# Second modulation, spectrum sums, last residual and shared product of the last batch on VectorE, with a new slot order

## The reference

```python
scores = jnp.einsum('bthd,bghd->bhtg', Q, K) / np.sqrt(DH)
topv, topi = jax.lax.top_k(scores, K_TOP)          # 32 of 1024, 4 heads
attn_mean = attn.mean(axis=1);  c_t = attn_mean @ V
x = layernorm(x_text, g_norm_in, b_norm_in)
x = x * (1.0 + mod_gate * scale_in) + mod_gate * shift_in      # "film in", from c_t
y = s4d(x, ...)                                                # long convolution by FFT
y = y * (1.0 + mod_gate * scale_out) + mod_gate * shift_out    # "film out"
xt = x_text + y
xt = xt + gelu(layernorm(xt, g_ffn, b_ffn) @ W1 + b1) @ W2 + b2
...                                                            # layernorm, then x + tanh(g) * (that)
top_id = jnp.argmax(x @ gate_w); score = sigmoid(max)          # 8 experts, one for each row
y = (silu(xs @ rt_gate[e]) * (xs @ rt_up[e])) @ rt_down[e]     # xs = x * score
shared = (silu(x @ sh_gate) * (x @ sh_up)) @ sh_down
x = x + tanh(g_ffn) * (shared + routed)
```

## Time and profile before

| | us |
|---|---|
| median of 3 runs | 1805.63 |
| lowest, highest | 1803.59, 1806.4 |
| the profiled execution | 1804.41 |
| its span (first to last instruction) | 1802.6 |

### The profile page before, as it was taken

The page is one execution under the profiler, slowest core; times in us unless marked ns, Lnnn a source line. Parts: engine busy times, 40 slices in busy tenths (PEclk is TensorE's granted clock), DMA queues, the critical chain, the costliest instruction groups (busy, mean ns, idle before and its releaser), DMA issues.

```text
span 1802.6 us, 20762 instructions
## 1 busy us (share of the span) xinstructions
PE 1409.9 (78%) x6269; PEld 987.7 (55%) x6269; DVE 1479.2 (82%) x2091; ACT 1111.9 (62%) x2366; POOL 1204.7 (67%) x1349
## 2 busy tenths in 40 slices
PE   6566658778876878679878878897788778878796
PEld 3233445455544555547565646564656465655796
DVE  7999999999999999889998999899989993103121
ACT  3689844856485648555976587658864775233442
POOL 1499838577856885697678958895789568515232
PEclk8666778879887988799999999898989989988898
DMA  7200120012102200122232222232223210843232
GB/s 214 59 5 2 39 68 31 24 45 56 25 12 49 50 24 7 47 83 76 76 83 65 73 72 71 62 88 74 59 65 87 55 53 22 266 121 105 62 51 27
DMA packets 96451, 115.16 MB, mean 64 GB/s; under 512 B 17840, under 2 KB 73144, under 8 KB 96196
## 3 DMA queue, kind: packets, MB, share of 16 engines
q1 hardware_dynamic: 84196, 99.26, 19.0%
q0 software_dynamic: 12144, 14.58, 5.1%
HBM read 75.48 MB, written 19.58 MB: 53 GB/s over the span
## 4 chain that ended last, share of the span: by engine, by line
DVE 52%; PE 15%; POOL 12%; issue 11%; ACT 7%; DMA 3%; SPq 1%; POOLq 0%; DVEq 0%
DVE R L1419 18%; DVE ZB L1422 15%; DVE ZB L1415 6%; DVE R L1411 6%; PE PS L1952 3%; DVE R L1376 2%; DMA out<-R 2%; ACT ZB L1009 2%; POOL ZB L725 2%; POOL R L904 2%; ACT R L1015 2%; PE PS L2063 2%; POOL R L898 1%; POOL xs_d L882 1%; PE PS L1971 1%
## 5 line engine op out<-in xcount | busy, mean ns | idle before, releaser
L1419 DVE MAX8 R<-ZB 128x8 f32<-128x1024 f32 x384 | 471.3, 1227 | 12.2
L1422 DVE MATCH_REPLACE8 ZB<-R,ZB 128x1024 f32<-128x1024 f32 x384 | 464.1, 1209 | 0.0
L1012 ACT ACTIVATE R<-PS 128x512 f32<-128x512 f32 (+6 forms) x412 | 181.8, 470 | 193.6 <-PE PS L2017 32.2
L725 POOL TENSOR_TENSOR ZB<-ZB 128x1024 f32<-128x1024 f32 x96 | 231.6, 2413 | 94.6 <-ACT ZB L1009 90.8
L727 POOL TENSOR_TENSOR ZB<-ZB 128x1024 f32<-128x1024 f32 x96 | 226.5, 2359 | 7.5
L1009 ACT ACTIVATE R<-R 128x32 f32<-128x32 f32 (+4 forms) x356 | 96.4, 275 | 196.9 <-DVE R L1419 172.1
L1411 DVE MAX8 R<-PS 128x8 f32<-128x1024 f32 x128 | 156.2, 1220 | 1.2 <-PE PS L1705 1.2
L1415 DVE MATCH_REPLACE8 ZB<-R,PS 128x1024 f32<-128x1024 f32 x128 | 155.4, 1214 | 0.0
L1015 ACT ACTIVATE R<-R 128x1 f32<-128x1 f32 (+1 forms) x384 | 140.7, 391 | 20.2 <-POOL R L712 15.2
L1009 ACT ACTIVATE ZB<-ZB,R 128x1024 f32<-128x1024 f32 x128 | 146.2, 1143 | 0.3 <-DVE ZB L1422 0.2
L1009 ACT ACTIVATE ZB<-PS,R 128x1024 f32<-128x1024 f32 x128 | 142.6, 1114 | 4.2
(11 more groups left out here) (247 smaller groups left out, 3048.1 us busy)
## 6 DMA issues: line engine op xcount, KB each, us to landing
ZR<-ZR SPq DMA_DIRECT2D x96, 128.0 KB
ZB<-in_L_ffn_rt_gate SPq DMA_DIRECT2D x21, 512.0 KB, 4.1
ZB<-in_L_ffn_rt_up SPq DMA_DIRECT2D x21, 512.0 KB, 5.0
ZB<-in_L_ffn_rt_down SPq DMA_DIRECT2D x21, 512.0 KB, 6.3
R<-in_x SPq DMA_DIRECT2D x16, 512.0 KB, 4.9
ZB<-in_ctx SPq DMA_DIRECT2D x8, 768.0 KB, 5.4
R<-xs_d SPq DMA_DIRECT2D x39, 128.5 KB, 2.2
out<-R SPq DMA_DIRECT2D x32, 128.0 KB, 1.7
```

The lines of the kernel that those rows point to most:

```text
L725: pool.tensor_tensor(e, e, w, ALU.subtract).then_inc(s.g_att, 1)
L1012: return act.activation(o, i, ACT.Copy, **k)
L1419: vec.max(ml[:, 8 * r:8 * r + 8], w).then_inc(s.v_tk, 1)
L1422: vec.match_replace(w, ml[:, 8 * r:8 * r + 8], w, NEG).then_inc(s.v_tk, 1)
```

## The change

For the last batch alone, POOL's film in, fold, spectrum sums, inverse sums, film out, residual and shared product are written into VectorE's program instead. They stand at the slots `DVE_LAST`. The shared product then reads its second factor out of PSUM, so ACT's four copies of it go; PE's SH_DOWN waits for these products by the banks that they free. The other batches keep the work on POOL. Besides, every slot table of every engine has new numbers; of these the diff shows five. Lines of the changed kernel are 1 to 3 higher up to 1544 and up to 69 higher behind.

```diff
-POOL_OUT = ((101, 101, 101.9, 102.8), (88.7, 88.8, 89.1, 89.3))
...
+POOL_OUT = (92.2, 92.2, 92.4, 95.2)
...
-ACT_SH = ((134.2, 135, 145.6, 145.6), (134, 134, 138.1, 161.5))
...
+ACT_SH = ((146.9, 147.4, 147.4, 147.7), (143, 161.7, 161.7, 161.7))
...
-DVE_ROUTE = ((118.3, 119.4), (123.3, 123.3))
...
+DVE_ROUTE = ((121.2, 123.6), (109.4, 112.3))
...
+DVE_LAST = (4, 8.5, 13.1, 28.9, 28.9, 45.2, 45.2, 45.2, 46, 46, 46, 47.2, 47.2, 50.2, 50.2, 82.4, 88.7, 88.7, 89.4, 132.3,
+            133.9, 133.9, 141)
...
+                    if b < B - 1:
+                        for i in range(4):
+                            yield at + POOL_FILM_IN[i]
...
+                    if b < B - 1:
+                        for i in range(4):
+                            yield at + POOL_OUT[i]
...
             def shared():
-                for b in range(B):
+                for b in range(B - 1):
                     for k in range(4):
-                        yield post_at(b) + POOL_SHUP[b == B - 1][k]
+                        yield post_at(b) + POOL_SHUP[k]
                         use = SHARED + 4 * (k // 2) + k % 2
...
+                    if b == B - 1:
+                        for i in range(4):
+                            yield at + DVE_LAST[i]
+                            fi = big[:, 4 + i, :]
+                            on.wait_ge(*q_done("post", b, FILM_IN + i))
+                            on.wait_ge(s.a_ln, 12 * b)
+                            for k in range(4):
+                                on.wait_ge(s_res[k], 16 * b)
+                            on.wait_ge(s.g_fi, n)
+                            t = own.then_inc(TT(u[:, i, :], xl[:, i, :], fi[:, 0:256], ALU.mult))
+                            on.wait_ge(own.sem, t)
+                            TT(u[:, i, :], u[:, i, :], fi[:, 256:512], ALU.add).then_inc(s.g_fi, 1)
+                        yield at + DVE_LAST[4]
+                        on.wait_ge(s.g_fi, n + 4)
+                        for i in range(4):
+                            on.wait_ge(s_acc[i], 16 * b)
+                        own.then_inc(TT(xt[:, 0:2, :], u[:, 0:2, :], u[:, 2:4, :], ALU.add))
+                        TT(xt[:, 2:4, :], u[:, 0:2, :], u[:, 2:4, :], ALU.subtract).then_inc(s.g_sd, 1)
                     for j in range(4):
                         yield at + DVE_SPECTRUM[b == B - 1][j]
...
+                        if b == B - 1:
+                            yield at + DVE_LAST[5 + j]
+                            on.wait_ge(*q_done("post", b, DFT + j))
+                            on.wait_ge(*q_run("post", b - 1, SH_DOWN + 3))
+                            on.wait_ge(s.g_y, n)
+                            own.then_inc(TT(yf[:, j, 0:256], q0[:, 0:256], q1[:, 256:512], ALU.subtract))
+                            TT(yf[:, j, 256:512], q0[:, 256:512], q1[:, 0:256], ALU.add).then_inc(s.g_y, 1)
...
+                    if b == B - 1:
+                        for i in range(2):
+                            yield at + DVE_LAST[9 + i]
+                            on.wait_ge(*q_done("post", b, INV + i))
+                            on.wait_ge(s.g_inv, n)
+                            TT(xt[:, i, :], qs[i][:, 0:256], qs[i][:, 256:512], ALU.add).then_inc(s.g_inv, 1)
+                            TT(xt[:, i + 2, :], qs[i][:, 0:256], qs[i][:, 256:512], ALU.subtract).then_inc(s.g_inv, 1)
+                        for i in range(4):
+                            yield at + DVE_LAST[11 + i]
+                            fo = big[:, i, :]
+                            on.wait_ge(*q_done("post", b, FILM_OUT + i))
+                            on.wait_ge(s.g_inv, n + 4)
+                            t = own.then_inc(TT(xt[:, i, :], xt[:, i, :], fo[:, 0:256], ALU.mult))
+                            on.wait_ge(own.sem, t)
+                            TT(xt[:, i, :], xt[:, i, :], fo[:, 256:512], ALU.add).then_inc(s.g_fo, 1)
                     yield at + DVE_MOMENTS[b == B - 1][0]
...
+                    if b == B - 1:
+                        for i in range(4):
+                            yield at + DVE_LAST[15 + i]
+                            z = tmp[i][:, 0:D]
+                            on.wait_ge(s.a_ln, 12 * b + 4 + i + 1)
+                            on.wait_ge(s.a_w, 4)
+                            on.wait_ge(s.g_z, n)
+                            t = own.then_inc(TT(z, z, gout, ALU.mult))
+                            on.wait_ge(own.sem, t)
+                            t = own.then_inc(TT(z, z, bout, ALU.add))
+                            on.wait_ge(own.sem, t)
+                            on.wait_ge(s.xr_in, 16 * b + 16)
+                            TT(x1[:, i, :], z, u[:, i, :], ALU.add).then_inc(s.g_z, 1)
...
+            def shared():
+                b = B - 1
+                for k in range(4):
+                    yield post_at(b) + DVE_LAST[19 + k]
+                    use = SHARED + 4 * (k // 2) + k % 2
+                    on.wait_ge(*q_done("post", b, use))
+                    on.wait_ge(*q_run("post", b, use + 2))
+                    TT(big[:, k, :], big[:, k, :], q_bank("post", b, use + 2), ALU.mult).then_inc(q_sem("post", b, use + 2), 1)
...
-            weave(setup(), attention(), prep(), weights(), kernel_rows(), post(), tiles(), routed())
+            weave(setup(), attention(), prep(), weights(), kernel_rows(), post(), shared(), tiles(), routed())
...
-                        on.wait_ge(s.g_sh, 4 * b + 4)
+                        if b < B - 1:
+                            on.wait_ge(s.g_sh, 4 * b + 4)
+                        else:
+                            for use in (2, 3, 6, 7):
+                                on.wait_ge(*q_done("post", b, SHARED + use))
```

More of the change, by code:

```diff
@@ L811, in post @@
-                    yield at + POOL_FOLD[b == B - 1][0]
-                    on.wait_ge(s.g_fi, 4 * b + 4)
-                    for i in range(4):
-                        on.wait_ge(s_acc[i], 16 * b)
-                    own.then_inc(pool.tensor_tensor(xt[:, 0:2, :], u[:, 0:2, :], u[:, 2:4, :], ALU.add))
-                    pool.tensor_tensor(xt[:, 2:4, :], u[:, 0:2, :], u[:, 2:4, :], ALU.subtract).then_inc(s.g_sd, 1)
-                    for j in range(4):
-                        yield at + POOL_SPECTRUM[b == B - 1][j]
-                        q0, q1 = qs[2 * (j % 2)], qs[2 * (j % 2) + 1]
-                        on.wait_ge(*q_done("post", b, DFT + j))
-                        if b:
-                            on.wait_ge(*q_run("post", b - 1, SH_DOWN + 3))
-                        own.then_inc(pool.tensor_tensor(yf[:, j, 0:256], q0[:, 0:256], q1[:, 256:512], ALU.subtract))
-                        pool.tensor_tensor(yf[:, j, 256:512], q0[:, 256:512], q1[:, 0:256], ALU.add).then_inc(s.g_y, 1)
@@ L1322, in shared @@
             def shared():
-                for b in range(B):
+                for b in range(B - 1):
                     for k in range(4):
-                        yield post_at(b) + ACT_SHUP[b == B - 1][k]
+                        yield post_at(b) + ACT_SHUP[k]
                         use = SHARED + 4 * (k // 2) + k % 2 + 2
```

222 lines of the change are left out of this document (112 added, 110 removed), and 8 rows, old and new, of the table POST_AT.

## The result

The changed kernel is slower: 1821.39 us median (1820.57 to 1823.29, four runs) against 1804.61 (1803.36 to 1806.4), a ratio of 1.0094 with a 95% interval of 1.0076 to 1.0111. I had forecast 1793, with 0.07 for slower. The profiled execution has a span of 1819.7 where it had 1802.6.

The account below looks back on a forecast made before the run. VectorE (82% busy) was taken to bound attention to 1507 us, then a chain through all engines. Main part -4.4 and tail -8.0 gave -12.4 from 1802.6, forecast 1793; own range 1788 to 1796, overall 1784 to 1801.

Parts of the forecast that it names:

- step 1: Route in batches 0 and 1: later gate and rank groups cover VectorE's waits of 2.15 and 1.24; -5.6 us.
- The rule that I set aside: GpSimd and VectorE share SBUF access, holding up two-SBUF-input instructions; would make the last residual 1.3 longer, left out.
- step 2: Batches 2 to 5, routing tables on POOL: sum 14 ahead of scaling starts 0.7 later per frame; net -0.3 us.
- Other slots: Main part, remaining slots moved by an instruction or two, first frame above all: +0.8 us, bounds -2 and +3.
- Rival C: Three POOL residual biases ahead of a sum wait for ACT's late tiles, stalling VectorE in seven frames: 1820, chance 0.08.
- The tail: Last batch after attention, work moved from POOL to VectorE: the end comes 8.0 us earlier.
- The fold: Tail, after the accumulate lands: on VectorE two adds take 1.4 to 1.5 with handoff instead of 2.64; -1.1 us.
- The residual: Tail, last residual: twelve adds take 5.5 on VectorE instead of 8.7 on POOL; -3.3 us at the second moments.
- Root and gate: Tail: ACT's last SiLU moves earlier, to just behind the moments, so root and gate come 7.0 us earlier.
- The shared part: Tail, shared product on VectorE: SH_DOWN waits less, though two matmul pairs need a freed bank; -3.5 us, bounds 0 and -5.5.
- rival D: Shared matmuls keep the higher clock throughout with fewer pauses ahead: 1788 us, chance 0.11.
- The late accumulates: Tail: three copies behind ACT's weight pick put three accumulates in a row before the first expert scatter: +2.5 us.

Follow-up runs that it names:

- run 5: Changed kernel with the route's gate group rewritten to read first operands from PSUM, intermediates in the gate's bank, no tensor_scalar: 1800.46 us, ratio 0.9967 to before.
- main_new: Kernel before with the changed kernel's slots for batches 0 to 6, old slots and old POOL work for the last batch: 1828.88 us, ratio 1.0121.
- route_late: Kernel before with only VectorE's route slots (DVE_ROUTE) of batches 0 to 6 set to the changed kernel's later ones: 1829.13 us, ratio 1.0125.
- gate_early: Changed kernel with the gate group of batches 0 to 6 back three attention instructions earlier, rank group left: 1819.73 us, ratio 1.0079.
- psum_route: Changed kernel, gate group computed from PSUM with fused compare-and-multiply operations, some tensor_scalars still reading SBUF: 1823.21 us, ratio 1.0089.
- probe_two: Kernel before plus one 128x8 VectorE add, both operands in SBUF, behind each attention tile's first MATCH_REPLACE8: 1866.83 us, one run.

## Why the prediction was wrong

1. **Route, step 1: the mechanism was half of it.** The waits went as forecast (3.4 a frame in batches 0 and 1, and their like later). The two groups of a route then took 5.6 in three frames and 6.8 in four, in place of 2.5 to 2.8. In batches 0 to 2 that leaves 0.3 to 0.6 of the 3.4 gained; in batches 3 to 5, which had 1.3 to 2.0 of wait to lose, the route costs 2.0 to 2.4 each. I had priced the moved instructions at their old durations. The step that failed is that one: "both should be covered by 1.2 us instructions". I asked what stood ahead of them on VectorE, not what POOL would run beside them at the new time. In its place the runs show two operations of each group held to the end of POOL's sum, 26.5 us in seven frames, and 21.0 us back once the gate group no longer had two operands in SBUF (run 5).
2. **The rule that I set aside.** The rule of the GPSIMD Engine Reference (section Specifications) in the Trainium skill, which names VectorE instructions with two SBUF inputs, or in a 2-port mode, stood in the prediction, weighed only for the tail's adds, where POOL has nothing to run and they did cost 0.42 to 0.43 (0.69 for the fold). The place where it decides was the main part, where POOL's order had just been moved as well. I priced it at 1.3 us, left that out of the sum, and it cost about 20. The row that I priced it by was misread too. The nine adds at 41.53 are not slowed to 0.56 each: the first lasts 1.36, since POOL's L795 runs to 42.61, and the eight behind it 0.43 each, with POOL idle. The merged row hid a hold behind a mean.

```profile
41.53 1.36 DVE L1376 TENSOR_TENSOR R<-R 128x256 f32<-128x256 f32 x1
```

```profile
41.29 1.32 POOL L795 TENSOR_TENSOR ZR<-R,ZR 128x512 fp32r<-128x512 f32 x1 [10.93 <-ACT R L1012]
```

3. **Tables, step 2.** The wait for POOL's last sum was forecast at about 17 and is 21.6. The new order of sum and scaling cost 1.4 to 1.8 in each of three frames where I had 0.7. Part is the hold again: in run 5 these intervals are 0.7 to 1.1 shorter.
4. **Other slots.** I took 0.8. In run 5, with most of the hold gone, attention ends 1.6 after that of before, where the forecast had it 4.4 ahead: 6.0 for everything else, of which the 4.7 of hold that is left there can be a part. That is also most of what run 5 lacks: it is 5.6 faster than before where I forecast 12.4. The intervals of the changed kernel show 3.8 in the first 16 tiles, 1.3 at the spectrum's products in two frames, 1.2 to 1.7 for PE's routed tile in three. How much of the first is the order and how much the start, which moved by 1 to 2 between executions, is open.
5. **Rival C, the L845 trio,** is real and small. The slack of 3.43 at that sum fell to 0.83, as the 2.7 that I charge say, and never below nothing. In one frame of seven a wait for a sum came one tile further on, L1418 for L726, 2.70.
6. **From the last route to the fold.** The landing of the last accumulate came 27.0 late (1567.05 after 1540.01) where attention was 19.6 late. The last route begins 26.9 late (1518.74 after 1491.87), since its gate group stands 1.1 behind the last tile's first MATCH_REPLACE8 where it stood 6.2 ahead. From there to the landing it is 48.3, before 48.1; without the hold at the gate group, in run 5, 44.6.
7. **The tail came as forecast or better.** Starts in the profiled executions, with `main_new` as the fair comparison (the same main part, the old tail):

| start of | before | changed | `main_new` | changed less `main_new` | forecast |
|---|---|---|---|---|---|
| DFT | 1542.7 | 1568.5 | 1568.3 | +0.2 | -1.1 |
| UP | 1582.6 | 1606.2 | 1608.3 | -2.1 | -1.6 |
| gate | 1644.4 | 1664.8 | 1669.9 | -5.0 | -7.0 |
| SH_DOWN | 1675.8 | 1688.8 | 1701.3 | -12.5 | -10.5 |
| first expert tile | 1686.8 | 1699.3 | 1712.2 | -12.9 | -10.5 |
| first scatter | 1712.7 | 1728.1 | 1739.7 | -11.5 | -8.0 |
| end | 1802.6 | 1819.7 | 1828.9 | -9.2 | -8.0 |

The accumulates landed 1.5 later in the changed kernel's execution than in that of `main_new` (1567.05, 1565.59). Counted from the landing each difference is 1.5 larger: 1.2 less at the DFT, 6.5 at the gate, 10.7 at the end.

The fold is 1.3 long and 1.5 with the handoff, as priced. The residual's twelve adds take 6.2 in place of 8.7; the last normalised tile comes 1.0 late behind a copy that waits for PE. The root begins right behind the SiLU, as forecast, and the SiLU came 0.9 after the moments' end where I had 0.3. (Root and gate are 6.6 by my own working, 1635.89 less 1629.3; I wrote 7.0.)

The shared part gained 7.5 between gate and SH_DOWN where I had 3.5, and the four more have a cause that I had not seen. VectorE must finish the route's tables before it takes the first product. It is free 18.7 after the gate matmul begins, in the kernel before 23.1. Of these 4.5, 2.9 are the held 128x1 add shown above: the seven adds take 1.32 where they took 4.19, since POOL has no shared products left to hold them. `main_new` has such a hold as well, 2.55 for an operation of 0.49, and is free after 20.8. The other 1.6 are rival D: the first eight shared passes ran in 5.07 at a granted clock of 0.72, before in 6.65. That isn't a gain of the moved work, since they ran so in `main_new` too:

```profile
1675.60:1680.40 4.80, 4.80 (x9) 0.72 0.26 31
```

The changed kernel's shared passes, and its SH_DOWN, which ran at 1.00 throughout, 32 passes in 7.17 (5.80 + 3.63 before):

```profile
1670.50:1675.40 4.90, 4.90 (x10) 0.72 0.01 3
...
1688.80:1695.90 7.10, 7.10 (x32) 1.00 0.41 101
```

What SH_DOWN gained, the first expert tile lost again to a wait for its rows, 1.93 and 0.71 for the DMA from xs_d: it is 12.9 ahead of `main_new` where SH_DOWN was 12.5. The late accumulates put the first scatter 28.8 behind the first expert matmul (forecast 28.5); the steps, 4.76 for 4.66, cost 1.6 more. What the moved work gives without the new slots of the last batch was not run apart.

## What to carry to other kernels

Where an instruction is moved on VectorE, read what POOL runs at the new time, and compare the durations of the same line through the trace: one that varies without cause (0.19, 0.41, 0.49; 0.16 and 3.03) is the sign. Take rows that merge several instructions apart first. A small operation with both operands in SBUF beside a long tensor_tensor of POOL costs up to the whole of that (2.96 of 3.02); with one operand in PSUM (0.20), or as a reduction (0.15), it isn't held. Work that is taken off POOL can so make VectorE faster where it isn't expected: 2.9 us in this tail. And a table of slots is one object: moving one entry of one engine to where the other set has it put a wait on PE into the program that neither set has (`route_late` 23 us, `gate_early` 3.4 a frame).

## What the runs showed of the hardware

- VectorE's tensor_tensor with two SBUF operands, and the tensor_scalar of `psum_route` on one, are held to the end of the POOL tensor_tensor that is running, to within 0.06 in the route. A longer one still has its own work to do then: the 128x256 add at 41.53 ends 0.28 after POOL's instruction. They hold VectorE as busy, not as waiting, and no list of waits shows it. A tensor_tensor or scalar_tensor_tensor with one operand in PSUM (0.16 to 0.20), a tensor_reduce from SBUF (0.15 to 0.19), MAX8 and MATCH_REPLACE8 (1.22 and 1.21 in either kernel) are not. The Trainium skill (GPSIMD Engine Reference, Specifications) has the rule for two SBUF inputs, and these traces agree. Whether the tensor_scalar ran in the 2-port mode that the page names besides, no run here shows.
- POOL is hardly slowed by it: 2.33 to 2.40 beside the held operations, 2.36 elsewhere. Where an add of `probe_two` and a POOL instruction began together to within 0.02, the add took 0.16 and POOL's lasted 0.02 to 0.05 longer (0.78 for 0.73).
- A 128x8 reduction between two dependent instructions of VectorE costs nothing.
